# Second self-attention layer: the values products of two steps of a chunk issued together, the first held back by a step

## What is computed

```python
xn = rmsnorm(x, norm_w)
q = (xn @ Wq).reshape(B, T_dec, H, hd)
k, v = split((encoder_out @ Wkv))                    # 77 context tokens
q_phi, k_phi = taylor(q @ Wqf), taylor(k @ Wkf)      # 1, x, x*x: (1 + s/2)^2 and so on
linear_out = (q_phi . sum_s k_phi v) / (q_phi . sum_s k_phi + 1e-6)
k_win, v_win = split(xn @ Wwin)
scores = q . k_win / sqrt(hd), only keys j with i - 64 <= j <= i
window_out = softmax(scores) @ v_win
x = x + concat(linear_out, window_out) @ Wout
```

## Time and profile before

| | us |
|---|---|
| median of 3 runs | 2232.75 (2230.76 to 2235.25) |
| the profiled execution's own time | 2233.14 |
| its span in the profile | 2231.3 |
| second layer's four batches in it | 130.5, 129.8, 134.2, 87.8 |

### The profile page before, as it was taken

How to read it: one execution, slowest core, us unless ns; L and a number is a source line. 1 busy time by engine, 2 the same in 40 slices (tenths; PEclk the granted TensorE clock), 3 DMA queues, 4 the chain that set the end, 5 groups by cost and what they waited for, 6 DMA issues and landing times. The chain is left out here.

```text
span 2231.3 us, 38605 instructions
## 1 busy us (share of the span) xinstructions
PE 2019.3 (90%) x14610; PEld 1327.2 (59%) x14610; DVE 1386.3 (62%) x3054; ACT 1137.3 (51%) x1750; POOL 768.4 (34%) x1012
## 2 busy tenths in 40 slices
PE   4999999999998879998999998998989998989989
PEld 2333433343342248876566575665677777888989
DVE  4876776676777756644545454452677784866655
ACT  2265456555545675551644645363545553555444
POOL 3023123213312353311633626244211201656656
PEclk8799999999998999998999999999999999999999
DMA  6705403510730000017460715420422210000000
GB/s 145 137 11 104 70 1 65 87 27 26 123 75 1 1 15 1 1 45 125 88 119 21 137 23 119 60 85 1 161 86 86 86 58 1 11 10 13 16 12 20
DMA packets 77774, 126.68 MB, mean 57 GB/s; under 512 B 16650, under 2 KB 34826, under 8 KB 77582
## 3 DMA queue, kind: packets, MB, share of 16 engines
q1 hardware_dynamic: 74966, 122.63, 26.2%
q10 hardware_dynamic: 2624, 1.58, 0.2%
HBM read 93.59 MB, written 30.32 MB: 56 GB/s over the span
## 5 line engine op out<-in xcount | busy, mean ns | idle before, releaser
L1099 DVE TENSOR_REDUCE nmx_causal<-banks 128x1 f32<-128x333 f32 (+4 forms) x896 | 435.2, 537 | 179.0 <-PE banks L830 177.2
L988 ACT ACTIVATE probs_causal<-banks 128x1024 f32<-128x1024 f32 (+5 forms) x384 | 331.1, 899 | 263.7 <-PE banks L855 259.6
L830 PE MATMUL banks<-ks_causal,qs_causal 96*128 96x333 bf16 (+4 forms) x896 | 271.9, 339 | 13.7 <-DVE nmx_causal L1099 7.6
L753 POOL TENSOR_SCALAR_AFFINE_SELECT probs_window<-probs_window 128x512 f32<-128x512 f32 (+1 forms) x272 | 161.8, 601 | 260.5 <-ACT probs_window L988 249.7
L753 POOL TENSOR_SCALAR_AFFINE_SELECT probs_causal<-probs_causal 128x512 f32<-128x512 f32 (+2 forms) x160 | 92.0, 575 | 461.1 <-ACT probs_causal L988 460.8
L855 PE MATMUL banks<-qs_causal,ks_causal 97*128 97x512 bf16 (+5 forms) x896 | 212.1, 332 | 20.4 <-ACT probs_causal L988 15.3
L1099 DVE TENSOR_REDUCE nmx_window<-banks 128x2 f32<-128x384 f32 (+2 forms) x320 | 142.8, 460 | 103.7 <-PE banks L830 100.0
L879 PE MATMUL banks<-probs_causal,v_causal 128*17 128x512 f32 (+5 forms) x1792 | 187.9, 493 | 0.0
L828 PEld LDWEIGHTS banks<-below,identb 128*128 128x128 bf16 x512 | 49.7, 98 | 174.4 <-DVE nmx_causal L1099 125.1
L988 ACT ACTIVATE probs_window<-banks 128x768 f32<-128x768 f32 (+2 forms) x128 | 99.7, 785 | 105.0 <-PE banks L855 104.4
L830 PEld LDWEIGHTS banks<-ks_causal,qs_causal 96*128 96x128 bf16 x896 | 86.6, 100 | 103.9 <-DVE nmx_causal L1099 60.9
(11 more groups left out here) (261 smaller groups left out, 4130.7 us busy)
## 6 DMA issues: line engine op xcount, KB each, us to landing
fs_masked<-in_fside SPq DMA_DIRECT2D x32, 616.0 KB, 3.7
ks_causal<-zk SPq DMA_DIRECT2D x96, 137.6 KB
ks_window<-zk SPq DMA_DIRECT2D x96, 137.6 KB
qs_causal<-zq SPq DMA_DIRECT2D x96, 128.0 KB
qs_window<-zq SPq DMA_DIRECT2D x96, 128.0 KB
zk<-parts_causal SPq DMA_DIRECT2D x24, 275.2 KB, 2.8
zk<-parts_window SPq DMA_DIRECT2D x24, 275.2 KB, 2.4
zq<-parts_causal SPq DMA_DIRECT2D x24, 256.0 KB, 7.1
```

The lines of the kernel that those rows point to most:

```text
L753: pool.affine_select(out=v, in_=v, compare_op=ALU.is_ge, fill=0.0, base=const, pattern=[[0, QH], [by_c, wd]], channel_multiplier=by_p).the ...
L830: ins = pe.matmul(bk[:, c:c + m], qs[q][0:KR, h, t * P:(t + 1) * P], ks[q][0:KR, h, key:key + m], start=cover is None, stop=True, skip_gro ...
L988: ins = act.activation(dst, src, ACT.Exp, scale=DH ** -0.5)
L1099: dve.tensor_reduce(dst, src, AX.X, ALU.max, negate=True).then_inc(emptied_v, 1)
```

## The change

In the second layer (`first` is false) a `values` token is not put down at once. It is kept in `held` until the next one comes, and then both are put down together. The last `values` of a chunk is never kept. All chunks of this layer have an even number of steps, so what comes is always a pair: S(n) S(n+1) V(n-2) V(n-1). No instruction is added or removed, on any engine.

```diff
     number = {one: n for n, one in enumerate(steps)}
+    held = []
...
                     if at >= 2 and (first or steps[at - 2][0] == b):
-                        main.append(("values", *steps[at - 2]))
+
+                        held.append(("values", *steps[at - 2]))
+                        if len(held) == 2 or steps[at - 2][3] == len(steps_of(steps[at - 2][2])) - 1 or first:
+                            main += held
+                            held = []
...
             if q + 1 == NQ and (b + 1 == B or not first):
+                main += held
+                held = []
                 main.append(("values", *steps[at - 1]))
```

## The result

The changed kernel takes **2244.39 us** (median of 6 runs, 2241.04 to 2252.36), the kernel before 2231.41 beside it: a ratio of 1.0054, 95% interval 1.0034 to 1.0074, 13.0 us slower. The prediction was 2233.0, within 2227 to 2239.

The account below looks back on a forecast made before the run. PE was taken as the bound where ring tokens and projections fill gaps, ACT at quad ends. Gains of 4.2 us against losses of 3.2 and 1.2 gave +0.2 on 2233.14, forecast as 2233.0, range 2227 to 2239.

Parts of the forecast that it names:

- The price of a pair: Two products standing together on PE save one switch from ring matmuls and one back, about 0.21 us.
- The gains at the ends of quads: Pairs, mostly at quad ends where ACT is the bound, were to gain 4.2 us in all.
- The hand walk: Following the list by record lengths and latencies: copy of OUT 0.3 us earlier at the end of batch 0's quad 2.
- 3 x 0.8 + 1.5: Gain of 0.8 us through quads 2 and 3 in each of batches 0 to 2, and 1.5 in batch 3.
- A: Start of quad 1, batches 0 to 2: `ke` copy falls behind the held exponential, PE stands still 1.15 us.
- B: Quad 1, 10 us later, batches 0 to 2: projection copies fall behind the exponential, PE stops 1.45 us, 1.0 more.
- what is given back: In quad 1, a 0.57 us bank wait and a shorter mask wait, leaving 1.06 us lost per batch, 3.2 in all.
- C: Start of quad 1's chunk 2, where PE waits for the copy of OUT; the prediction does not have this place.
- place 3: End of quad 1: masks go ahead of a 1.09 us subtraction on POOL, shortening PE's 0.98 us wait for them.
- The shift's DMA: In batch 2 the loads end about 1 us later against it: 1.2 us lost, nothing in the other batches.
- The clock: Stretches of PE at half clock: taken as 0, with 3 us either way; stops in quad 1 speak for more.
- The second: Rival, chance 0.3: the held exponential stops the bank ring in quad 1, 5.0 to 8 us slower, 2238 to 2241.

Follow-up runs that it names:

- moved_four: Kernel before with only each pair's first product moved behind the scores of step e+3, plus a fourth `probs` buffer: 2224.60 us, ratio 0.9968.
- late: The change, holding products back only from quad 2 of batches 0 to 2 and in all of batch 3: 2236.76 us, ratio 1.0010 to before.
- moved_only: Kernel before with only each pair's first product moved, half way between the scores of step e+3 and the second product: 2233.12 us, ratio 1.0000.
- fix_c: The change, with the scores of step 1 of quad 1's chunk 2 put back behind the subtraction `middle`: 2241.37 us, ratio 1.0029 to before.
- early: The change, holding products back only in quads 0 and 1 of batches 0 to 2: 2247.52 us, ratio 1.0060 to before.
- four_before: Kernel before, its order kept, with a fourth `probs` buffer in the second layer: 2234.17 us, ratio 0.9989.

## Why the prediction was wrong, step by step

**The price of a pair** was right. 0.21 us was predicted from a pitch of 0.34 against 0.45, and 3.87 us for 19 pairs measure 0.20. That it comes through whole in one order (`moved_four`) was to be expected only where PE doesn't wait, and in none of the orders with three buffers did it.

**The gains at the ends of quads, 4.2 us, were wrong, in sign too.** The hand walk had 1.5 us gained in batch 3; 1.42 were lost, 0.4 of it to the clock. It had 0.8 gained in each other batch; `late` loses 0.35 in batch 1. The term that failed is "3 x 0.8 + 1.5", and the step in it is the end of the held exponential. The walk did hold it behind its product and had it end at 1130.75, 0.06 earlier than before. The row of before:

```profile
1130.21 0.60 ACT L988 ACTIVATE probs_window<-banks 128x512 f32<-128x512 f32 x1 [0.84 <-PE banks L855]
```

and those of the change:

```profile
1129.73 0.96 PE L886 MATMUL banks<-probs_window,v_window 128*17 128x192 f32 x24
1130.48 0.60 ACT L995 ACTIVATE probs_window<-banks 128x512 f32<-128x512 f32 x1 [0.99 <-PE banks L886]
```

In the change it ends at 1131.08, 0.27 later than before and 0.33 later than predicted. The product that it waits for is the first 16 of the 24 records, and it stands behind the transposes and the next scores now, so it starts at 1129.73. The rest of the walk moved by the same amount: the products between the squares start at 1131.69 where I had 1131.3, the second square and the copy of OUT behind them are late by 0.4, and the gain of 0.3 became a loss of 0.1. For batch 3, `moved_four` against `moved_only` shows what the wait costs in that order: 3.3 us.

**A and B, 3.2 us net, had the right mechanism and the wrong size.** The stops were as worked out: 1.15 at A (1.17 by its own terms) against 1.12 idle (1.20 by the starts) measured, 1.45 at B against 1.31 (1.49 by the starts). The term that failed is what is given back: the prediction's own parts (1.15, 1.0 more than before at B, and 0.2) add up to 2.35 per batch, from which I had subtracted 0.57 and the wait for masks and was left with 1.06. Next to nothing was given back. A became 1.63: putting its token back takes 1.06 of that, and most of the rest is a `ke` token that waits 0.56 us for ACT's copy `xnT`, which nothing in the prediction has. B became 1.37. Together they are 3.0 a batch, 9.0 in all instead of 3.2.

**C was missed**, 0.74 per batch net, 1.31 against the same order with C put back. The prediction looked at one new order on POOL, the masks of step 3 of chunk 2 ahead of a subtraction, and counted it as a help. The wait of 0.98 for these masks is indeed gone. It did not see that 7 us earlier another pair is swapped, ahead of where the list of place 3 starts: the masks of step 1 now stand ahead of a subtraction (1239.07 and 1240.51, before 1234.46 and 1233.35). ACT's next copy waits for that subtraction, and behind that copy stands the copy of OUT. `fix_c` shows that they are two swaps: it undoes the one at C, and the wait for the masks of step 3 does not come back.

**The shift's DMA, 1.2 us, did not come.** The scores that wait for it in batch 2 stand for 2.2 us, against 2.32 in the earlier trace rows. Over the layer PE's waits for it are 4.7 us, before 4.5.

**The clock.** One slow stretch more lies in batch 1, and one more behind the end of the layer (granted 0.52 from 1536.8 to 1543.6, where before has 1.00 behind its own end). I had said that the stops at A and B speak for more such stretches, and the trace doesn't agree: the 6.8 us behind A, B and C in batch 1 are all at 1.00, and the slow stretch there comes ahead of A, at the end of a stop of 1.06 us for DVE. The span of the profiled execution can't be used for the size of the loss for that reason; the places can.

**The rivals.** The second was the right one, with its condition met (a loss of over 2.5 us per batch around quad 1: it is 3.7), and its price of 5 to 8 us still too low, since it kept the 4.2 us of gain and had no C. The range ended at 2239 because the gain was subtracted in every case. A case in which the hold cancels the gain and nothing is given back, 6.6 + 1.2 = 7.8, was worked out in its parts and never added up; it would have given 2240.5, still 4 us short.

## What to carry to other kernels

Where a planner places other work by its index in a list, holding one token back moves all of that work against the tokens behind it: list every pair of instructions on each in-order engine whose order is swapped, on ACT and POOL too, and ask of each who waits for the one that is now second. A wait that is hidden in one order is a stop in another: with the copies ahead of the held exponential PE goes on at once (`moved_only` at A and B), and with one token per place moved so that they, or the masks, stand behind it, 1.1 to 1.3 us are lost each time. And look for a spare of the buffer that a change makes live longer: the third-buffer wait cost 7 us even in the better orders. With the fourth buffer, and all else left in its place, 62 pairs gave 7 us, where the change with its 43 pairs, three buffers and the rest moved lost 13.

## What the runs showed of the hardware

A change between matmuls of the two tile shapes has a price: 19 round trips saved were 3.87 us in a stretch of 86 (`moved_four`). That is one order; 12 and 23 saved gave 0.65 and 0.30 in two others, so the runs don't show that it adds up. The Trainium skill (TensorEngine Tiling (Array Packing), Key Properties) says that changing the tiling mode drains the engine; the trace agrees and puts about 0.20 us on a way there and back. The products are also float32 behind bf16 matmuls, and on the way over, rows of the kernel before tell the two apart:

```profile
1232.65 0.25 PE L830 MATMUL banks<-ks_window,qs_window 96*128 96x192 bf16 x1
1232.73 1.91 PE L802 MATMUL banks<-xnT_window,w_window 128*128 128x512 f32 x4
...
1234.56 0.25 PE L830 MATMUL banks<-ks_window,qs_window 96*128 96x192 bf16 x1
1234.74 0.63 PE L879 MATMUL banks<-probs_window,v_window 77*17 77x256 f32 x8
```

A float32 projection over 128 columns of the array starts 0.08 us behind a bf16 ring matmul, the usual pitch, and a product over 17 columns 0.18 behind. So the type is not what costs the extra 0.1. The way back has no such pair of rows here.

Beside that I had not expected how exactly one execution repeats another: with the same order and the same clock, batch 3 took 86.14 us in the kernel before, 86.13 in `early` and 86.13 in `four_before`, so a trace resolves 0.1 us at a place where the time of the whole kernel resolves 4 us.
